# Reordering the prologue and one step of the per-chunk work in a two-part graph network kernel

## The chip, the cores and the metric

The kernel runs on one core of a Trainium2 chip. The metric is the device time of one execution in microseconds. The engines are named as in the profile: PE (TensorE; PEld is its weight load), DVE (VectorE), ACT (ScalarE), POOL (GpSimd) and SP (SyncE, which here only issues transfers). Each engine runs its own instructions in the order in which they are written; between engines there are only semaphore waits.

## What is computed

For each of 64 graphs of 128 nodes with 128 features (all float32), two blocks follow each other:

```
x1  = layernorm(x + L0(x, adj))          # L0: graph convolutions on nodes 0..24 only
out = layernorm(x1 + L1(x1, adj) * mask)

L0: w = softmax(fusion_w)
    for 5 groups g of nodes: A = adj_g + I, deg = rowsum(A), Ahat = deg^-1/2 A deg^-1/2
        h     = relu(Ahat (x_g W1[g]) + b1[g])
        out_g = relu(Ahat (h   W2[g]) + b2[g]);   fused[nodes of g] += w[g] * out_g
L1: A = (adj != 0); h = x1
    for 5 layers l: h = GRU( A^T (h weight[l]), h )      # gates r, z, n; w_ih, w_hh shared
```

## The kernel before

**Tiling.** The 64 graphs are cut into 4 chunks of 16, a chunk into 4 visits of 4 graphs (512 columns). L0 is done for a chunk at a time, L1 for a visit at a time. The main loop has 80 windows: 20 for each chunk (5 layers times 4 visits, the four visits in turn). `w.i` is the number of a window in its chunk (0 to 19). While the loop does L1 of one chunk, L0 of the next chunk is spread over its windows; class `Plan` says which step is done in which window. L0 of chunk 0 has no loop to hide in and stands in the prologue.

**A window.** PE multiplies the state of a visit by the hidden weights and the neighbours' sum by the fused weights `wf`, each as three products (high half by high half, low by high, high by low: L1063 to L1065), transposes the state that the window before the last has left (`turn`, L1050) and sums neighbours for a window to come (`aggregate`, L1057). ACT does the sigmoids and tanh and the high halves, POOL `dg` (L433), DVE `cg` (L889, L892), the new state `hT` (L830, L832) and the low halves (L818, L824). `turn` waits for the state of the window before the last, which DVE writes behind its L889 and L892 of the window before.

**L0 of a chunk, step by step.** DVE adds the adjacency rows up (`degrees`), POOL takes the power -1/2 (`power`), DVE scales (`scaled`), DVE (chunk 0) or POOL (`spread`) lays the block-diagonal matrices `bda` and `bdb` out. PE transposes them (`adjacency`), multiplies by x (`neighbours`), by W1 (`hidden_a`, `hidden_b`), by W2 (`second_a`, `second_b1`, `second_b2`) and by the adjacency again (`output_a`, `output_b`), ACT and DVE taking each result out of PSUM. `gather` adds the groups' parts into `fused` in 8 tensor_tensor instructions, each waiting for the one before it (DVE in the prologue, L746; POOL in the loop, L382). `back` transposes `fused` to rows (PE, L1026), `add` adds them to x (DVE, L756), and layer norm 1 follows: statistics on DVE (`norm1`, L763, L767), deviation on POOL (`deviation1`, L395 to L400), and the scaling on ACT, in the prologue for visit 0 half on DVE (`half_norm1`, L781) and for visits 2 and 3 on POOL. `ones` (POOL, L368) turns 4 graphs' adjacency in place into 0/1, from the 1 MB of `an` that SP loads for each chunk; the same loads bring `xn`.

**The prologue's weights.** `w_ih`, `w_hh` and `weight` are loaded, transposed on PE and copied by ACT (`wit`, `wh`, `wlt`). PE then multiplies `wlt[l]` by `wit` to give the fused weights of layer l (`fused_weights`, L936) in PSUM bank `WF_BANKS[l]`; ACT copies their high half (`high_weights`, L474), DVE subtracts for the low half (`low_weights`, L773). The loop uses banks P0 and P1 at once, P4 to P7 for states and sums. The softmax of `fusion_w` needs an exponential on ACT, whose activation tables hold either the exponential or the sigmoid; a tiny sigmoid (L560) loads the second set ahead of the loop.

**Orders by hand.** Every engine's prologue is a written-out list of these steps. SP issues the rows of `adj` and `x` for chunk 0, W1, W2, then chunk 0's `xn` and `an`, then the rows of `adj` for chunk 1. ACT issues its share of rows and then `w_ih`, `w_hh`, `weight`, the biases, the mask and `fusion_w`.

Of the kernel before, what the change touches and what calls it, by code (L numbers as in the profile page):

```python
# [7 lines left out]
NG = len(GROUPS)  # L8
# [70 lines left out]
class Plan:  # L79

    ADJ, Y, HA, HB, SA, SB, OA, OB, GATHER, BACK, REST = 2, 3, 4, 5, 6, 7, 8, 9, 10, 11, (12, 13)
    DEGREES, SCALED, SPREAD = 10, 12, 13
# [3 lines left out]
    STATS2 = {4: 0, 6: 1, 8: 2, 9: 3}  # L86
# [33 lines left out]
def build(nc, x, adj, nodemask, W1, b1, W2, b2, fusion_w, weight, w_ih, w_hh, b_ih, b_hh, out):  # L120
# [3 lines left out]
    with ctx:  # L124
# [75 lines left out]
        WF_BANKS = (1, 5, 6, 7, 0)  # L200
# [8 lines left out]
        def b1c(g, c):  # L209
# [4 lines left out]
        w_in, wl_in, w1_in, w2_in, xt_in, xt_pool_in, xa_in = map(sem, (  # L214
            "w_in", "wl_in", "w1_in", "w2_in", "xt_in", "xt_pool_in", "xa_in"))
# [62 lines left out]
        def _(sp):  # L278
# [4 lines left out]
            sp.dma_start(w1[:], W1.rearrange("g d h -> d g h")).then_inc(w1_in, 16)  # L283
# [39 lines left out]
        def _(pool):  # L323
# [103 lines left out]

# [20 lines left out]
        def _(act):  # L448
# [110 lines left out]
            high_weights(1)  # L559
            nc.scalar.activation(fmx[:], fmx[:], ACT.Sigmoid)  # L560
# [3 lines left out]
            for l in range(2, LAYERS):  # L564
                high_weights(l)
# [75 lines left out]
        def _(dve):  # L641
# [142 lines left out]
            degrees(0)  # L784
            dve.wait_ge(prep_hi, 1)
            TT(wh[:, 1, :], P[1][:, 0:GATES], wh[:, 0, :], ALU.subtract).then_inc(prep_lo, 1)
            scaled(0)
            adjacency(0)
            dve.wait_ge(w_in, 16 * 6)
            nc.vector.tensor_reduce(fmx[:], fw[:], AX.X, ALU.max, negate=True).then_inc(fw_ok, 1)  # L790
            neighbours(0)
            dve.wait_ge(exp_ok, 1)
            link(nc.vector.reciprocal(fsum[:], fsum[:]))
# [4 lines left out]
            hidden_b0(0)  # L798
            low_weights(0)
            second_b1(0)  # L800
            second_b2(0)
            low_weights(1)
            degrees(1)
            gather(0)
# [384 lines left out]
```

## Time and profile before

| | |
|---|---|
| median of 3 runs | 569.48 us (569.06 to 569.87) |
| the profiled execution | 569.57 us |
| its span in the profile | 567.3 us |
| busy: PE, DVE, ACT, POOL | 516.9, 443.0, 370.7, 257.7 us |
| mean granted TensorE clock | 0.97 of 2.4 GHz |
| loop: first product of window 0 | 52.01 us |

The span is divided into what each engine was busy with; an engine that is idle while another one sets the pace costs nothing. A row of a timeline gives start and duration in us, and in brackets the idle time of the engine before it and what ended it. The chain that ended last is followed back from the last instruction, so its rows in order of time tell what set the pace.

### The profile page before, as it was taken

Reading aid. Unit: us, or ns where it says so; the run is one execution under the profiler, and the core shown is the slowest. Engines: PE = TensorE matmul, PEld = TensorE weight load, DVE = VectorE, ACT = ScalarE, POOL = GpSimd, SP = SyncE. Lnnn points to the kernel's source line nnn. Section 1 sums busy time; section 2 is a strip of 40 time slices with the busy share of each in tenths; the row PEclk is TensorE's granted clock in tenths of the full one; section 3 lists DMA queues with packets and bytes.
Section 4 is the critical chain, followed back from the end, with each engine's and each line's share of the span. In section 5 each row is a group of like instructions: output and inputs, shape, how many; then the busy total and the mean of one; then the engine's idle time right before and its main releaser. Section 6 shows DMA issues by size and latency. Waiting matters only on the chain.

```text
span 567.3 us, 8362 instructions
## 1 busy us (share of the span) xinstructions
PE 516.9 (91%) x2907; PEld 434.7 (77%) x2907; DVE 443.0 (78%) x970; ACT 370.7 (65%) x682; POOL 257.7 (45%) x303
## 2 busy tenths in 40 slices
PE   1945999999999999998999999998999999999981
PEld 1734889887788788886788788887888888888860
DVE  3474667679998876888998877786998898887785
ACT  1433765675786765676787666676887767788644
POOL 5356523554554224666463323665254234442325
PEclk9985999999999999999999999998999999999995
DMA  4948610000000000000100000000000000000002
GB/s 106 233 134 198 155 27 8 1 1 0 1 1 1 1 25 7 20 1 20 39 1 1 0 1 2 20 0 20 18 20 2 1 1 1 19 20 27 12 0 74
DMA packets 35712, 17.27 MB, mean 30 GB/s; under 512 B 4429, under 2 KB 35648, under 8 KB 35672
## 3 DMA queue, kind: packets, MB, share of 16 engines
q1 hardware_dynamic: 33225, 15.78, 10.7%
q10 hardware_dynamic: 2063, 0.80, 0.6%
q8 instruction: 23, 0.38, 0.3%
q0 software_dynamic: 384, 0.17, 0.2%
q14 instruction: 17, 0.14, 0.1%
HBM read 12.54 MB, written 4.19 MB: 30 GB/s over the span
## 4 chain that ended last, share of the span: by engine, by line
PE 79%; DVE 8%; POOL 5%; ACT 3%; issue 2%; ACTq 1%; DMA 1%; POOLq 0%; DVEq 0%
PE p L1063 17%; PE p L1065 17%; PE p L1064 17%; PE p L1057 11%; PE p L1050 7%; PE p L981 3%; PE p L955 1%; POOL fused L382 1%; POOL an L368 1%; DVE cg L889 1%; PE p L974 1%; DVE cg L892 1%; DVE hT L832 1%; DMA zg<-in_L_gnn_weight_dram 1%; DVE dg L830 1%
## 5 line engine op out<-in xcount | busy, mean ns | idle before, releaser
L433 POOL TENSOR_TENSOR dg<-hT,ng 128x512 f32<-128x512 f32 x80 | 126.0, 1575 | 266.8 <-ACT ng L625 266.8
L1063 PE MATMUL p<-hhi,wh 128*128 128x512 f32 x240 | 102.3, 426 | 0.0
L889 DVE SCALAR_TENSOR_TENSOR cg<-p,biasc,rg 128x512 f32<-128x512 f32 x80 | 59.6, 745 | 54.5 <-ACT rg L612 54.1
L1063 PE MATMUL p<-ghi,wf 128*128 128x512 f32 x240 | 102.0, 425 | 0.0
L1064 PE MATMUL p<-hlo,wh 128*128 128x512 f32 x240 | 95.2, 397 | 0.0
L1065 PE MATMUL p<-hhi,wh 128*128 128x512 f32 x240 | 95.1, 396 | 0.0
L1065 PE MATMUL p<-ghi,wf 128*128 128x512 f32 x240 | 95.0, 396 | 0.0
L1064 PE MATMUL p<-glo,wf 128*128 128x512 f32 x240 | 95.0, 396 | 0.0
L612 ACT ACTIVATE rg<-p,gb 128x512 f32<-128x512 f32 x80 | 55.4, 693 | 33.5 <-PE p L1065 27.7
L818 DVE TENSOR_TENSOR hlo<-hT,hhi 128x512 fp32r<-128x512 f32 x76 | 72.4, 953 | 3.5 <-ACT hhi L636 0.6
L625 ACT ACTIVATE ng<-cg,biasc 128x512 f32<-128x512 f32 x80 | 57.9, 723 | 23.8 <-DVE cg L892 23.6
L1057 PEld LDWEIGHTS p<-an,nat 128*128 128x128 f32 x512 | 67.0, 191 | 5.8
L623 ACT ACTIVATE zg<-p,gb 128x512 f32<-128x512 f32 x80 | 55.0, 687 | 24.8 <-PE p L1065 24.6
L1057 PE MATMUL p<-an,nat 128*128 128x128 f32 x512 | 67.4, 274 | 0.0
L892 DVE TENSOR_TENSOR cg<-cg,p 128x512 f32<-128x512 f32 x80 | 55.0, 688 | 8.3
L824 DVE TENSOR_TENSOR glo<-p,ghi 128x512 fp32r<-128x512 f32 x80 | 55.3, 691 | 5.8 <-ACT ghi L581 5.8
L832 DVE TENSOR_TENSOR hT<-ng,dg 128x512 f32<-128x512 f32 x80 | 55.5, 694 | 2.8
L610 ACT COPY nat<-p 128x512 f32<-128x512 f32 x64 | 37.9, 592 | 28.8 <-PE p L1050 27.6
L1050 PE MATMUL p<-ident,hT 128*128 128x128 f32 x320 | 50.1, 280 | 6.9 <-DVE hT L832 6.9
L830 DVE TENSOR_TENSOR dg<-zg,dg 128x512 f32<-128x512 f32 x80 | 55.0, 688 | 0.0
L1065 PEld LDWEIGHTS p<-hhi,wh 128*128 128x128 f32 x240 | 45.3, 189 | 11.1
L1065 PEld LDWEIGHTS p<-ghi,wf 128*128 128x128 f32 x240 | 45.3, 189 | 11.0
(128 smaller groups left out, 832.8 us busy)
## 6 DMA issues: line engine op xcount, KB each, us to landing
xn<-in_x_dram SPq DMA_DIRECT2D x8, 512.0 KB, 5.2
an<-in_adj_dram SPq DMA_DIRECT2D x8, 512.0 KB, 7.1
out_dram<-xn SPq DMA_DIRECT2D x16, 256.0 KB, 2.3
w<-in_L_gnn_W_dram SPq DMA_DIRECT2D x2, 640.0 KB, 5.4
xt<-in_x_dram SPq DMA_DIRECT2D x16, 50.0 KB
zg<-in_L_gnn_weight_dram ACTq DMA_DIRECT2D x1, 320.0 KB, 5.6
xt<-in_x_dram SPq DMA_DIRECT2D x8, 36.0 KB
xt<-in_x_dram SPq DMA_DIRECT2D x12, 24.0 KB
```

What stands on the lines that cost most here:

```text
L433: nc.gpsimd.tensor_tensor(dg[:, w.k % 2, :], hT[:, w.slot, :], ng[:, w.k % 2, :], ALU.subtract).then_inc(d_ok, 1)
L625: nc.scalar.activation(ng[:, p, :], cg[:, p, :], ACT.Tanh, bias=bin_).then_inc(n_ok, 1)
L818: TT(hlo[:, m % SLOTS, :], hT[:, m % SLOTS, :] if source is None else source[:], hhi[:, m % SLOTS, :], ALU.subtract).then_inc(lo_ok, 1)
L830: TT(dg[:, p, :], zg[:, p, :], dg[:, p, :], ALU.mult).then_inc(e_ok, 1)
L832: TT(hT[:, s, :], ng[:, p, :], dg[:, p, :], ALU.add).then_inc(h_ok, 1)
L889: STT(cg[:, p, :], PH[:], bhn, rg[:, p, :], ALU.add, ALU.mult).then_inc(t1_ok, 1)
L892: TT(cg[:, p, :], cg[:, p, :], PI[:], ALU.add).then_inc(c_ok, 1)
L1050: last = TR(bank[:, q * 128:(q + 1) * 128], src(q), ident[:])
L1057: last = MM(bank[:, q * N:(q + 1) * N], src(q), an[:, b + q, :], start=True, stop=True)
L1063: MM(bank[:], w[:, 0, cols], xhi, start=start, stop=False)
L1064: MM(bank[:], w[:, 0, cols], xlo, start=False, stop=False)
L1065: return MM(bank[:], w[:, 1, cols], xhi, start=False, stop=stop)
```

## The change

`Plan`: `back` moves from window 11 to 12, the rest of `add` from 12 and 13 to 13 and 14, `degrees` (and `power`) from 10 to 11, `scaled` from 12 to 13, `spread` from 13 to 14, and one statistics step of layer norm 2 from window 9 to 10.

Prologue, by engine:
- SP no longer issues W1; ACT issues it behind `weight`. POOL issues the mask. ACT issues `fusion_w` first. The waits are split: PE's first transposes wait for `w_ih` and `w_hh` alone.
- ACT does the exponential and the tiny sigmoid first, then the copies; `high_weights(0)` goes behind `second_a(0)`, `high_weights(1)` to (4) behind `output_b(0)`; `maskc` is copied behind `second_a(0)`.
- DVE takes the low half of `wh` behind `adjacency(0)`; the `low_weights` go between and behind the steps of `add` and `norm1`, one behind `lo_state(0)`; `scaled(1)` goes behind `norm1(3)`.
- POOL does `ones(0)` and `ones(1)` ahead of `power(1)`, `ones(2)` and `ones(3)` behind it, `spread(1)` last.
- PE transposes `wl` and the biases' rows behind `adjacency(0)`; `fused_weights(0)` goes behind `second_b2(0)`, (1) and (2) behind `output_b(0)`, (3) and (4) behind `back(0)`.

```diff
-    ADJ, Y, HA, HB, SA, SB, OA, OB, GATHER, BACK, REST = 2, 3, 4, 5, 6, 7, 8, 9, 10, 11, (12, 13)
-    DEGREES, SCALED, SPREAD = 10, 12, 13
+    ADJ, Y, HA, HB, SA, SB, OA, OB, GATHER, BACK, REST = 2, 3, 4, 5, 6, 7, 8, 9, 10, 12, (13, 14)
+    DEGREES, SCALED, SPREAD = 11, 13, 14
...
-    STATS2 = {4: 0, 6: 1, 8: 2, 9: 3}
+    STATS2 = {4: 0, 6: 1, 8: 2, 10: 3}
...
-        WF_BANKS = (1, 5, 6, 7, 0)
+        WF_BANKS = (1, 0, 5, 4, 7)
...
@@ sync
-            sp.dma_start(w1[:], W1.rearrange("g d h -> d g h")).then_inc(w1_in, 16)
...
@@ gpsimd
             power(0)
             spread(0)
+            pool.dma_start(maskr[:], nodemask).then_inc(mask_in, 16)
             pool.wait_ge(ac_zero, 2)
             load_adj_rows(pool, 1, TA, ac_pool_in[1])
+            ones(0)
+            ones(1)
             power(1)
-            spread(1)
-            for visit in range(SLOTS):
-                ones(visit)
+            ones(2)
+            ones(3)
             deviation1(0)
             deviation1(1)
             for visit in (2, 3):
                 deviation1(visit)
                 norm1(visit)
+            spread(1)
...
@@ scalar, loads
+            act.dma_start(fw[:], fusion_w.partition_broadcast(128)).then_inc(fw_in, 16)
+            act.dma_start(wir, ...).then_inc(gates_in, 16)
+            act.dma_start(whr, ...).then_inc(gates_in, 16)
             act.dma_start(wl, weight.rearrange("l c e -> c l e")).then_inc(wl_in, 16)
+            act.dma_start(w1[:], W1.rearrange("g d h -> d g h")).then_inc(w1_in, 16)
...
@@ scalar, steps (new order)
+            act.wait_ge(fw_ok, 1); exp; sigmoid
+            copy wit; copy wh high (prep_hi)
+            adjacency(0)
+            copy wlt (wlt_ok); copy biasc (prep_a)
+            neighbours(0); hidden_a(0); hidden_b1(0); second_a(0)
+            copy maskc; high_weights(0)
+            output_a(0); output_b(0)
+            high_weights(1..4)
...
@@ vector (new order)
+            degrees(0)
+            dve.wait_ge(fw_in, 16); reduce max of fw (fw_ok)
+            scaled(0)
+            adjacency(0)
+            dve.wait_ge(prep_hi, 1); wh low (prep_lo)
+            dve.wait_ge(exp_ok, 1); reciprocal; fw scaled
+            neighbours(0); gb; fb2 (b_ok)
+            hidden_b0(0); second_b1(0); second_b2(0)
+            degrees(1)
+            gather(0)
+            low_weights(0)
+            add(0, True); norm1(0)
+            low_weights(1)
+            add(0, False); half_norm1(0, HALVES[1])
+            low_weights(2)
+            norm1(1)
+            low_weights(4)
+            lo_state(0, PL)
+            low_weights(3)
+            lo_neighbours(0, PG)
+            norm1(2); norm1(3)
+            scaled(1)
+            lo_state(1, PM)
...
@@ tensor (new order)
+            pe.wait_ge(gates_in, 32); transposes of wir, whr
+            adjacency(0)
+            transposes of wl (wait wl_in); transpose of rows (wait w_in, wlt_ok)
+            neighbours(0); hidden_a(0); hidden_b(0); second_a(0)
+            transpose of maskr
+            second_b1(0); second_b2(0)
+            fused_weights(0)
+            output_a(0); output_b(0)
+            fused_weights(1); fused_weights(2)
+            back(0)
+            fused_weights(3); fused_weights(4)
```

The lists of ACT, DVE and PE above stand for the moved lines; the helpers that they call are unchanged. The waits of `prep_lo` on PE follow the new order of the low halves.

## Rows read from the trace of the kernel before

**Rows 1.** Busy time of each engine in the profile's page, with shares and instructions.

```profile
PE 516.9 (91%) x2907; PEld 434.7 (77%) x2907; DVE 443.0 (78%) x970; ACT 370.7 (65%) x682; POOL 257.7 (45%) x303
```

**Rows 2.** Timeline of PE: start, us, instruction; in brackets idle before, releaser.

```profile
13.54 1.06 PE L925 MATMUL p<-ident,zg 128*128 128x128 f32 x4
...
49.22 1.09 PE L1050 MATMUL p<-ident,xn 128*128 128x128 f32 x4 [12.61 <-ACT xn L532]
...
260.26 0.66 PE L1026 MATMUL p<-ident,fused 128*128 128x128 f32 x4 [2.25 <-POOL fused L382]
...
389.35 1.06 PE L1026 MATMUL p<-ident,fused 128*128 128x128 f32 x4 [2.08 <-POOL fused L382]
```

**Rows 3.** The chain that ended last, in order of time: start, us, what.

```profile
15.25 1.48 DVE bda L696 x4
...
18.42 1.33 PE p L936 x2
...
38.77 7.59 POOL an L368 x4
...
48.24 0.89 ACT xn L532 x2
...
52.01 0.59 PE p L1063
```

**Rows 4.** Timeline of DVE in the prologue.

```profile
14.29 0.56 DVE L786 TENSOR_TENSOR wh<-p,wh 128x384 fp32r<-128x384 f32 x1 [4.80 <-ACT wh L465]
...
31.08 0.38 DVE L672 TENSOR_TENSOR am<-ac,member 128x225 f32<-128x225 f32 x1
...
33.37 2.47 DVE L746 TENSOR_TENSOR fused<-fused,part 128x72 f32<-128x72 f32 x8 [0.56 <-ACT part L522]
...
36.73 1.21 DVE L756 TENSOR_TENSOR xn<-xn,p 25x128 f32<-25x128 f32 x4
...
39.29 2.29 DVE L756 TENSOR_TENSOR xn<-xn,p 25x384 f32<-25x384 f32 x4
```

**Rows 5.** Stretches of whole windows: busy (x count) by engine, clock, DMA share, GB/s.

```profile
121.96:168.78 46.82, 46.40 (x248) 36.95 (x246) 44.28 (x97) 32.44 (x57) 26.40 (x35) 1.00 0.00 1
249.93:298.00 48.07, 45.81 (x248) 37.05 (x246) 43.97 (x97) 36.71 (x69) 28.52 (x40) 1.00 0.06 18
379.16:428.10 48.94, 46.86 (x247) 38.80 (x246) 42.03 (x89) 36.56 (x69) 23.89 (x33) 0.97 0.06 17
501.83:540.54 38.71, 38.71 (x213) 32.65 (x212) 30.37 (x43) 29.87 (x52) 11.13 (x7) 1.00 0.07 21
151.83:168.78 16.95, 16.95 (x94) 13.64 (x92) 15.90 (x43) 13.54 (x27) 10.42 (x17) 1.00 0.00 1
...
384.91:394.79 9.88, 7.80 (x37) 6.43 (x36) 5.57 (x12) 5.05 (x10) 4.81 (x9) 0.83 0.10 28
```

**Rows 6.** Timelines of POOL and of SP's queue in the prologue.

```profile
9.49 1.83 POOL L338 TENSOR_TENSOR dinv<-deg,minus_half 128x9 f32<-128x9 f32 x1 [2.00 <-DVE deg L681]
...
19.97 7.14 SPq L246 DMA_DIRECT2D ac<-in_adj_dram  x8
```

**Rows 7.** Timeline of ACT in the prologue.

```profile
14.63 0.59 ACT L467 COPY cg<-p 128x512 f32<-128x512 f32 x1 [0.37 <-PE p L925]
...
30.59 1.28 ACT L560 ACT_TABLE_LOAD   x1
```

**Rows 8.** Short stretches ahead of and in window 0, with columns as in rows 5.

```profile
26.00:27.00 1.00, 1.00 (x12) 1.00 (x11) 0.12 (x1) 0.60 (x3) 0.00 (x0) 1.00 0.13 13
...
52.01:54.95 2.94, 2.94 (x8) 2.28 (x8) 2.25 (x12) 2.61 (x6) 0.23 (x2) 0.50 0.91 208
54.95:60.11 5.16, 5.16 (x37) 4.59 (x35) 2.87 (x9) 3.55 (x6) 4.65 (x11) 1.00 0.08 9
```

**Rows 9.** Timelines of POOL and DVE in window 1 of chunk 2.

```profile
193.84 1.63 POOL L433 TENSOR_TENSOR dg<-hT,ng 128x512 f32<-128x512 f32 x1 [3.72 <-ACT ng L625]
...
194.25 1.77 DVE L818 TENSOR_TENSOR hlo<-hT,hhi 128x512 fp32r<-128x512 f32 x1
```

More of the change, by code:

```diff
@@ L563, in _ @@
             output_b(0)
-            for l in range(2, LAYERS):
+            for l in range(1, LAYERS):
                 high_weights(l)
@@ L782, in half_norm1 @@
                 last.then_inc(ln1_dve, 1)
[L784 to L793, printed above, removed]
-            link(TS(fw[:], fw[:], fsum[:], None, ALU.mult))
-            dve.wait_ge(prep_a, 1)
-            TT(gb[:], biasc[:, BI:BI + 2], biasc[:, BI + 3:BI + 5], ALU.add)
-            TT(fb2[:], biasc[:, NG * HC:BI], fw[:], ALU.mult).then_inc(b_ok, 1)
[L798 to L804, printed above, removed]
-            scaled(1)
-            low_weights(2)
-            add(0, True)
-            norm1(0)
-            add(0, False)
-            half_norm1(0, HALVES[1])
-            norm1(1)
-            low_weights(3)
-            low_weights(4)
             def lo_state(m, source=None):
@@ L852, in norm2 @@
                 last.then_inc(ln2_st, 1)
+            degrees(0)
+            dve.wait_ge(fw_in, 16)
+            nc.vector.tensor_reduce(fmx[:], fw[:], AX.X, ALU.max, negate=True).then_inc(fw_ok, 1)
+            scaled(0)
+            adjacency(0)
+            dve.wait_ge(prep_hi, 1)
+            TT(wh[:, 1, :], P[1][:, 0:GATES], wh[:, 0, :], ALU.subtract).then_inc(prep_lo, 1)
+            dve.wait_ge(exp_ok, 1)
+            link(nc.vector.reciprocal(fsum[:], fsum[:]))
+            link(TS(fw[:], fw[:], fsum[:], None, ALU.mult))
+            neighbours(0)
+            dve.wait_ge(prep_a, 1)
+            TT(gb[:], biasc[:, BI:BI + 2], biasc[:, BI + 3:BI + 5], ALU.add)
+            TT(fb2[:], biasc[:, NG * HC:BI], fw[:], ALU.mult).then_inc(b_ok, 1)
+            hidden_b0(0)
+            second_b1(0)
+            second_b2(0)
+            degrees(1)
+            gather(0)
+            low_weights(0)
+            add(0, True)
+            norm1(0)
+            low_weights(1)
+            add(0, False)
+            half_norm1(0, HALVES[1])
+            low_weights(2)
+            norm1(1)
+            low_weights(4)
             lo_state(0, PL)
+            low_weights(3)
             lo_neighbours(0, PG)
@@ L1029, in _ @@
             adjacency(0)
-            pe.wait_ge(prep_lo, 1)
-            fused_weights(0)
+            pe.wait_ge(wl_in, 16)
+            for l in range(4):
+                last = TR(P[2][:, l * 128:(l + 1) * 128], wl[:, l, :], ident[:])
+            last.then_inc(prep_t, 1)
+            TR(P[3][:, 0:128], wl[:, 4, :], ident[:]).then_inc(prep_t, 1)
+            nr = NG * HC + NG + 6
+            pe.wait_ge(w_in, 16 * 4)
+            pe.wait_ge(wlt_ok, 1)
+            TR(P[3][:, 128:128 + nr], rows[:], ident[0:nr, 0:nr]).then_inc(prep_t, 1)
             neighbours(0)
@@ L1125, in _ @@
                 if k == 0:
+                    pe.wait_ge(prep_lo, 5)
                     enter(1, PM)
```

61 lines of the change are left out of this document (27 added, 34 removed).

## The prediction

> **What bounds the kernel now.** I read the page's busy shares first: PE is busy 516.9 of 567.3 us [rows 1], so a gain must come from stretches in which PE stands idle. I then listed PE's idle stretches by their releaser [rows 2]. Before the loop PE first idles about 12 us, then works until 36.6 us, and then idles 12.61 us until ACT has normalised the first visit. In the loop it waits 2.25 and 2.08 us at `back` (L1026) for the additions of `gather` on POOL; at the first chunk's `back` it does not wait. Third, the chain of waits in order of time [rows 3]: it goes through DVE's `bda`, the product of layer 0's weights on PE, and from 38.77 on through four `ones` on POOL (7.59 us) and the deviation behind them, until ACT starts on `xn` at 48.24. So before the loop POOL's order sets the end. Fourth, DVE's own order [rows 4] shows what comes into play once POOL is out of the way. Last, windows 10 to 17 of each chunk in the loop [rows 5], since the change moves steps among them.
>
> **The changed prologue.** All times are new positions on the old clock.
>
> DVE now waits 4.80 us for ACT's `wh`, only to subtract it, ahead of `scaled(0)` [rows 4]. POOL's `power(0)` ends at 9.49 + 1.83 = 11.3 [rows 6]. With the subtraction moved behind, `scaled(0)` runs from 11.4 to 13.35: 1.95 us, as from 14.8 (behind `wh`) to 16.73 [rows 3, 4]. PE's `adjacency(0)` takes 1.7 us (16.73 to 18.42 [rows 3]), so to 15.0. What is new between it and `neighbours(0)`: the transposes of `wl`, 1.06 and about 0.3 us [rows 2], ACT's copies of them (0.59 us and a shorter one, about 0.8 with waits [rows 7]) and the transpose of the rows: 2.2 us, to 17.2. It was 18.42 + 1.33 = 19.75 [rows 3], so 2.5 us are gained. Against that, `fused_weights(0)` (0.7) now stands ahead of `output_a`, in the place that `fused_weights(1)` had: nothing. ACT's table load of 1.28 us, at 30.59 right before `output_a` [rows 7], moves into the time before 13 us, where ACT waits anyway. The first addition of `gather(0)` can then start at 33.37 - 2.5 - 1.28 = 29.6 instead of 33.37 [rows 4]; `output_b` on PE, 2.5 us earlier, and ACT's first `part` behind it make it 30.0, and I keep 0.8 for a slow start of PE: 30.0 to 30.8.
>
> The order before `gather(0)` on DVE is still `degrees(1)`. Its rows of `adj` are issued by SP from 19.97 to 27.11 [rows 6]; W1's 640 KB leave SP for ACT's queue, which puts SP 0.5 to 2 us ahead, so they land at 26.5 to 28.1. DVE is free at 27.7 to 28.5. So `degrees(1)` is ready at about 28.1 and needs 1.75 us (31.08 to 33.37 less the 0.56 idle [rows 4]).
>
> POOL: chunk 0's loads end at about 26.4 (DMA share 0.13 in the slice from 26 [rows 8]). W1 out of their way takes up to 2 us off; I take 25.0. `ones(0)`, `ones(1)` at 7.59/4 = 1.9 each end at 28.8, `power(1)` (1.83 like `power(0)` [rows 6]) waits for `degrees(1)`, and `ones(2)`, `ones(3)` come after. Without contention they end at 35.5, before DVE has the statistics, so POOL is off the chain.
>
> **The cost the trace hardly shows.** `degrees(1)` and `gather(0)` are tensor_tensor with both inputs in SBUF, and they now run beside `ones`, where before POOL was idle or in a `pow` of 9 columns. The nearest row: a DVE tensor_tensor with two SBUF inputs that starts 0.41 us into a POOL tensor_tensor takes 1.77 us and ends 0.55 us after it [rows 9]: it is held until POOL's instruction is over. For `ones`, with one input, no row shows a DVE instruction of this kind starting inside. Lower bound: no hold, `gather` runs 30.8 to 33.2. Upper bound: each is held for all that is left of a `ones`. I take the hold, since the row is of the same engines and the same direction. Then `degrees(1)` runs 28.9 to 30.65 and `power(1)` 30.6 to 32.4; five or six of the eight additions are done by then, one is held by `ones(2)` to 34.4, and since each addition waits for the one before it, POOL takes `ones(3)` next, to 36.5. The last two end at 36.8, not 33.2: 3.6 us given back. Bounds for this end: 35.4 (loads at 24.2) and 38.0 (loads at 26.4).
>
> The Trainium skill ("SBUF — State Buffer", section "Who interferes with whom") says that DVE and GpSimd share a port pair as an exclusive lock, that a DVE instruction with two SBUF inputs contends with any GpSimd instruction that reads SBUF, and that whoever starts first blocks the other for the whole instruction. By that rule `ones` belongs with the held case; the trace agrees for tensor_tensor with its 1.77 us, and shows nothing for `ones`.
>
> Behind the additions: from their end 0.9 us to `add` (33.37 + 2.47 = 35.84 to 36.73), which covers `back` and `low_weights(0)`; then to the end of `add(0, False)` 39.29 + 2.29 - 36.73 = 4.85, and 0.5 for `low_weights(1)`, which now stands between [rows 4]. So DVE comes to its half of `norm1(0)` at 36.8 + 6.25 = 43.05, where it started at 48.24. POOL's deviation (46.4 to 48.24, 1.8 us) starts after the statistics at 40.3 and ends at 42.1: hidden. Now DVE is the last, not POOL. From there DVE's work to `lo_state(0)` is the same amount (one half norm, `norm1(1)`, two `low_weights`), so the first product of window 0 comes 3.8 us later as now (48.24 to 52.01 [rows 3]), at 46.9 instead of 52.01: **-5.1 us**. `low_weights(3)` (0.5) fits DVE's wait for `ghi`. `scaled(1)` and `spread(1)` (2.4 on POOL, ahead of window 0's `dg`) end ahead of `adjacency(1)` in window 2; `dg` is late by some 0.5 us for DVE, which has waits of over 1 us there: **+0.2**, at most 1.
>
> PE restarts at 1.2 GHz as now: the granted clock is 0.50 until 54.95, 5.7 us after the restart [rows 2, 8], and PE's idle time ahead of it remains some 5 us. A rise earlier or later by some us costs half of that: +-1.5 for the range.
>
> **The loop.** A window in which nothing is late takes 38.71/7 = 5.53 us. Windows 10 to 17 would take 8 x 5.53 + 0.5 for `back` = 44.7; they took 46.82, 48.07 and 48.94 [rows 5]. DVE's own work in a window is 4.5 us: in windows 15 to 17, 16.95/3 = 5.65 with the 1.2 of a norm1 (add's start to 39.29 less its 1.21 is 1.35 with gaps) [rows 4, 5]. Where a window's DVE work passes about 5.6, PE ends up waiting for hT at the turning of the next one. So I added up each window's DVE work and let PE wait for what it is late. `back` a window later removes both waits for POOL, 2.25 and 2.08, and the half clock behind the second (window 11 took 9.88 us at 0.83 [rows 5]; 5.53 + 0.5 + 2.08 = 8.1 at full clock): 6.0 us. But the same DVE work is now pushed into fewer windows: window 10 has only a norm2 or nothing, and window 14 has half of the rest of `add` (1.15) and a norm1 (1.2), 6.85 us in all, for which PE waits 1.3. `spread` in window 14 behind POOL's deviation (2.8 us) also makes `dg` and the next deviation 0.7 late, through ACT's norm1 and zg 0.4 for PE, and about 0.3 by holding DVE. Window by window: chunk 1: 5.75, 5.53, 6.03, 5.71, 6.15, 6.86, 5.68, 6.06 = 47.8 (+1.0); chunk 2: 5.75, 5.67, 6.17, 5.74, 6.15, 6.86, 5.68, 6.06 = 48.1 (0); chunk 3, without `degrees` and `scaled`: 5.75, 5.67, 6.03, 5.53, 5.53, 6.47, 5.68, 5.68 = 46.3 (-2.6). With 0.3 twice for `spread`: **-1.0 us**; bounds -6.0 (nothing given back) and +1.5. The other moves (a norm2 from window 9 to 10) lie in waits of over 1 us.
>
> **Sum.** -5.1 + 0.2 - 1.0 = -5.9. The profiled execution took 569.57 (span 567.3, 2.3 around it), the median is 569.48: **563.6 us**.
>
> **Rivals.**
> - *No hold by `ones`.* Additions end at 33.2, half norm at 39.45, window 0 at 43.3: -8.7 + 0.2 - 1.0, 560.0 us. For it: `pow` beside the additions did not hold them. Against it: rows 9. Chance 0.17.
> - *The waits at `back` vanish and nothing is given back*: 569.5 - 5.1 + 0.2 - 6.0 = 558.6 with the hold. Against it: 5.65 in windows 15 to 17 shows DVE at its limit. Chance 0.08.
> - *DVE is held at every turn*, loads as late as now, and chunk 1's windows slow down as bounded: additions end at 38.0, -3.9 + 1 + 1.5: 568.1. Chance 0.05 (with a part beyond the bound of 0.2%).
> - *The slower side: the clock.* If after the restart PE stays at 1.2 GHz for more windows, each costs up to its 5.53 us once more, since PE is busy throughout it: about 5. From 1.2 such windows on the gain of 5.9 is gone; two give 573.6. Against it: the same instructions raised it after 5.7 us. Chance 0.04.
> - The forecast, 0.66; within it earlier or later loads and clock.
>
> **Range and chances.** 558.5 to 567.0 takes in the first two rivals and leaves out about 1 in 10. The forecast's own range is 561.5 to 566. A difference of 0.2% (1.1 us) is about what a measurement of this kernel tells from none. Faster 0.93, within 0.03, slower 0.04.
>
> **What would show it.** Right: `bda` ends near 13.4; `neighbours(0)` starts on PE near 17.2; one or two of DVE's additions in the prologue take 1 to 2 us, ending with a `ones`; DVE, not POOL, ends the wait before `norm1(0)`; window 0's first product near 47; no PE idle ahead of `back` in the loop; window 15 near 6.9. Wrong: additions all below 0.4 us (first rival); window 15 at 5.6 (second); a granted clock of 0.50 past 53 us (fourth); or `neighbours(0)` waiting for `xt`, which W1 on ACT's queue could make late: it is due at 17.2.

## The result, and the profile after

The changed kernel takes 564.61 us (median of 4 runs, 564.47 to 564.89), the kernel before, run beside it, 569.53 us: a ratio of 0.9901 (95% interval 0.9877 to 0.9926; it isn't the quotient of the two medians, which is 0.9914). The forecast was 563.6. The profiled execution of the changed kernel took 564.52 us, its span is 562.6.

The busy line of its page answers to [rows 1]:

```profile
PE 519.8 (92%) x2907; PEld 434.3 (77%) x2907; DVE 447.4 (80%) x970; ACT 371.0 (66%) x682; POOL 259.5 (46%) x304
```

PE's timeline after the change, with the columns of [rows 2]:

```profile
17.59 0.29 PE L1027 MATMUL p<-ident,rows 21*128 21x21 f32 x1 [1.34 <-DMA rows<-in_L_gnn_b_hh_dram]
17.81 2.03 PE L944 MATMUL p<-na,xt 100*128 100x100 f32 x8
...
21.76 2.65 PE L953 MATMUL p<-ya,w 128*128 128x400 f32 x4
...
36.69 0.63 PE L1015 MATMUL p<-ident,fused 128*128 128x128 f32 x4 [2.24 <-DVE fused L747]
...
43.41 1.09 PE L1052 MATMUL p<-ident,xn 128*128 128x128 f32 x4 [3.98 <-DVE xn L782]
...
46.23 0.77 PE L1065 MATMUL p<-hhi,wh 128*128 128x512 f32 x1
...
63.35 0.52 PE L933 MATMUL p<-ident,bda 100*100 100x100 f32 x4 [1.64 <-DVE hlo L788]
```

The 12.61 us that PE waited for ACT [rows 2] have become 3.98 us for DVE. Window 0's first product starts at 46.23; in this view it started at 51.84 before (the chain of [rows 3] puts it at 52.01). The waits of 2.25 and 2.08 us at `back` are gone: the loop has no idle time of PE there any more. What came in instead is the last row: 1.64 us in window 2.

DVE's timeline (`add` is L757, `gather` L747, `half_norm1` L782, the state hT L802):

```profile
31.08 0.38 DVE L673 TENSOR_TENSOR am<-ac,member 128x225 f32<-128x225 f32 x1
...
33.74 2.80 DVE L747 TENSOR_TENSOR fused<-fused,part 128x72 f32<-128x72 f32 x8 [0.94 <-ACT part L515]
...
37.43 1.22 DVE L757 TENSOR_TENSOR xn<-xn,p 25x128 f32<-25x128 f32 x4 [0.42 <-PE p L1015]
...
42.68 0.58 DVE L782 TENSOR_SCALAR xn<-xn,rs,nm 128x128 f32<-128x128 f32 x2
...
60.37 1.67 DVE L802 TENSOR_TENSOR hT<-ng,dg 128x512 f32<-128x512 f32 x1
```

POOL's timeline (`ones` is L367, `power` L337, the end of `spread` L358, `dg` L435):

```profile
27.03 3.85 POOL L367 TENSOR_SCALAR an<-an 128x512 f32<-128x512 f32 x2 [10.49 <-DMA an<-in_adj_dram]
32.81 1.83 POOL L337 TENSOR_TENSOR dinv<-deg,minus_half 128x9 f32<-128x9 f32 x1 [1.92 <-DVE deg L682]
34.63 3.81 POOL L367 TENSOR_SCALAR an<-an 128x512 f32<-128x512 f32 x2
...
56.83 1.55 POOL L358 TENSOR_TENSOR bdb<-am,ksel 72x144 f32<-72x144 f32 x5
58.32 1.28 POOL L435 TENSOR_TENSOR dg<-hT,ng 128x512 f32<-128x512 f32 x1
60.03 1.45 POOL L435 TENSOR_TENSOR dg<-hT,ng 128x512 f32<-128x512 f32 x1 [0.42 <-ACT ng L626]
```

`gather` lies wholly beside `power` and `ones`, as foreseen, and yet its eight additions take 2.80 us instead of 2.47: they are not held for a whole `ones`.

Stretches of whole windows, with the columns of [rows 5]: windows 0 and 2, then windows 10 to 17 ahead of chunk 1, 15 to 17 of these, and 10 to 17 ahead of chunks 2 and 3:

```profile
46.23:53.85 7.62, 7.62 (x43) 6.61 (x43) 5.89 (x23) 6.15 (x12) 5.12 (x13) 0.89 0.82 216
...
59.38:67.45 8.07, 6.43 (x43) 5.33 (x41) 6.53 (x12) 5.46 (x12) 1.68 (x2) 1.00 0.71 186
117.18:165.93 48.75, 46.95 (x248) 36.91 (x246) 45.87 (x97) 32.51 (x57) 26.91 (x35) 1.00 0.00 1
146.76:165.93 19.17, 17.77 (x94) 13.49 (x92) 18.22 (x48) 13.62 (x27) 13.07 (x21) 1.00 0.00 1
247.09:295.97 48.88, 47.09 (x247) 36.86 (x246) 46.46 (x105) 36.79 (x69) 29.34 (x40) 1.00 0.06 17
377.13:423.46 46.33, 45.76 (x247) 37.25 (x246) 43.50 (x97) 36.70 (x69) 24.03 (x33) 1.00 0.06 18
```

Against the 46.82, 48.07 and 48.94 of [rows 5] that is +1.93, +0.81 and -2.61: the loop as a whole comes out even. The difference of the two spans splits as follows: prologue 51.84 to 46.23, -5.61; window 0 from 8.27 to 7.61, -0.66; window 2 from 6.59 to 8.07, +1.48; windows 10 to 17, +0.13. Together -4.66, of the 4.7 between 567.3 and 562.6. So between these two executions all of the gain is the prologue's, and the plan brings nothing. Experiment 2 adds a reservation to the second half, and experiments 1 and 5 show that the prologue's share is understated here.

### The profile page after: what moved, and what is told of

It reads as the page before. It is cut to its first block, busy times and chain, and to the rows that moved or that the text cites. A ratio compares the mean times of both kernels' runs of the same rounds, so it can differ in the third digit from the quotient of the medians.

```text
span 562.6 us, 8366 instructions
## 1 busy us (share of the span) xinstructions
PE 519.8 (92%) x2907; PEld 434.3 (77%) x2907; DVE 447.4 (80%) x970; ACT 371.0 (66%) x682; POOL 259.5 (46%) x304
## 4 chain that ended last, share of the span: by engine, by line
PE 68%; DVE 16%; POOL 6%; ACT 4%; issue 3%; ACTq 2%; DMA 1%; DVEq 0%; POOLq 0%
PE p L1065 14%; PE p L1067 14%; PE p L1066 14%; PE p L1059 9%; PE p L1052 6%; PE p L970 3%; DVE hT L802 2%; DVE cg L889 2%; DVE cg L892 2%; DVE xn L757 2%; DVE dg L800 2%; PE p L944 2%; PE p L963 1%; DMA rows<-in_L_gnn_b_hh_dram 1%; POOL dg L435 1%
## 5 line engine op out<-in xcount | busy, mean ns | idle before, releaser
L435 POOL TENSOR_TENSOR dg<-hT,ng 128x512 f32<-128x512 f32 x80 | 125.3, 1566 | 264.5 <-ACT ng L626 264.5
L788 DVE TENSOR_TENSOR hlo<-hT,hhi 128x512 fp32r<-128x512 f32 x76 | 75.8, 998 | 3.8 <-ACT hhi L637 0.6
L802 DVE TENSOR_TENSOR hT<-ng,dg 128x512 f32<-128x512 f32 x80 | 56.5, 706 | 2.8
L1052 PEld LDWEIGHTS p<-ident,hT 128*128 128x128 f32 x320 | 37.4, 143 | 23.8 <-DVE hT L802 18.8
L1065 PEld LDWEIGHTS p<-hhi,wh 128*128 128x128 f32 x240 | 45.6, 190 | 13.0 <-DVE cg L889 3.6
L1067 PEld LDWEIGHTS p<-hhi,wh 128*128 128x128 f32 x240 | 45.3, 189 | 11.0
```

The source lines that it names most:

```text
L435: nc.gpsimd.tensor_tensor(dg[:, w.k % 2, :], hT[:, w.slot, :], ng[:, w.k % 2, :], ALU.subtract).then_inc(d_ok, 1)
L788: TT(hlo[:, m % SLOTS, :], hT[:, m % SLOTS, :] if source is None else source[:], hhi[:, m % SLOTS, :], ALU.subtract).then_inc(lo_ok, 1)
L802: TT(hT[:, s, :], ng[:, p, :], dg[:, p, :], ALU.add).then_inc(h_ok, 1)
L1052: last = TR(bank[:, q * 128:(q + 1) * 128], src(q), ident[:])
L1065: MM(bank[:], w[:, 0, cols], xhi, start=start, stop=False)
L1067: return MM(bank[:], w[:, 1, cols], xhi, start=False, stop=stop)
```

## The experiments

The kernel before took 569.8 us beside experiments 1 to 4 (its executions range from 569.22 to 574.15), 570.17 beside 5 to 8 and 569.75 beside 9 to 12. Ratios are to it.

**1 and 2. Each half alone.** The kernel before with the new `Plan`, and the changed kernel with the old one (`STATS2` goes with it).

```diff
-    GATHER, BACK, REST = ..., 10, 11, (12, 13)      # experiment 1; experiment 2 is the other way round
-    DEGREES, SCALED, SPREAD = 10, 12, 13
+    GATHER, BACK, REST = ..., 10, 12, (13, 14)
+    DEGREES, SCALED, SPREAD = 11, 13, 14
```

> The kernel before with the new Plan alone; its prologue is untouched. If the loop's account of the trace after holds (windows 10 to 17 of the three chunks +1.9, +0.8 and -2.6 us), the change of the loop is worth nothing by itself: 569.6 us, within 0.5 of before. If instead the removed waits at back are a gain that something of the new prologue took away again, it takes 563.5 to 565.

> The changed kernel with the old Plan. If the parts add up, the prologue is the whole gain: 564.5 us, with the waits of 2.2 and 2.1 us ahead of back in the loop again and window 0's first product near 46.2. If the prologue needs the new Plan (a slower first chunk), 567 or more.

The plan alone: 572.09 us, 1.0023 (0.9996 to 1.0051), which is not told apart from no change, though the median is 2.3 us above the one expected at most 0.5 away. The prologue alone: 565.45 us, 0.9909 (0.9877 to 0.9942), where 564.5 was expected. With the plan alone windows 10 to 17 take 48.77, 48.88 and 46.33 us, as in the changed kernel: +0.15 in all, and the profiled execution is longer than the kernel before only by its prologue, whose instructions are the same. There window 0 starts at 53.82 instead of 51.84. PE's timeline of experiment 1 shows why:

```profile
19.46 1.87 PE L955 MATMUL p<-na,xt 100*128 100x100 f32 x8
21.12 2.33 PE L955 MATMUL p<-nb,xt 72*128 72x72 f32 x10
23.25 2.44 PE L964 MATMUL p<-ya,w 128*128 128x400 f32 x4
...
53.82 0.77 PE L1063 MATMUL p<-hhi,wh 128*128 128x512 f32 x1
```

In the kernel before the same three rows take 1.64, 1.28 and 1.54 us. By these durations PE came up to its full clock some 4 us later: in the kernel before at about 20.8, here at about 25.1. So an execution's prologue can be 2 us longer or shorter with no change to the code ahead of it, and that difference must not be read as an effect of the plan.

The same holds for the prologue's gain. The kernel before was profiled in an execution in which the clock rose at about 20.8, the changed kernel in one in which it rose at about 24.0, so the -5.61 compares an early rise with a late one. Of the profiled executions, experiment 1 (the old prologue, rise at about 25.1) is matched by experiment 5, whose edit acts only behind the start of window 0 and whose clock rose at about 25.0. PE's timeline of experiment 5:

```profile
21.71 2.93 PE L953 MATMUL p<-ya,w 128*128 128x400 f32 x4
24.43 2.22 PE L963 MATMUL p<-yb,w 128*128 128x144 f32 x16
...
46.67 0.76 PE L1065 MATMUL p<-hhi,wh 128*128 128x512 f32 x1
```

53.82 against 46.67: with the rise at the same time, the new prologue is worth 7.15 us. This is one execution of each; at which time the clock rose in the others isn't known.

In experiment 2 window 0 starts at 46.34. Its loop keeps both waits at `back`, and the clock was at half behind both of them, where in the kernel before it was so behind the second alone:

```profile
256.00:260.00 4.00, 4.00 (x15) 3.35 (x14) 1.88 (x5) 2.04 (x4) 2.57 (x2) 0.57 0.00 0
...
385.50:389.50 4.00, 3.71 (x14) 3.30 (x15) 1.13 (x4) 1.01 (x2) 1.46 (x2) 0.57 0.00 0
```

Windows 10 to 17 ahead of chunk 2 take 49.13 there instead of 48.07, and the three groups together 144.86, 0.90 more than in the changed kernel. The new plan takes the waits and the half clock behind them away: the changed kernel runs at 1.00 from 47.9 to 549.7 us. So the plan costs 0.13 us against an execution with one such stretch and saves 0.9 against one with two. The medians (565.45 and 564.61, intervals overlapping) don't decide what it is worth on average.

**3. `spread` a window earlier.**

```diff
-    DEGREES, SCALED, SPREAD = 11, 13, 14
+    DEGREES, SCALED, SPREAD = 11, 13, 13
```

> The changed kernel with spread back in window 13, all else as changed. Windows 15 to 17 take 19.2 us in chunk 1 and 19.2 in chunk 2, but 17.9 in chunk 3, which has no spread. Theory: spread behind POOL's deviation in window 14 costs that difference, so they fall to 17.9: 562.1 us. Rival: the difference is DVE's lateness from degrees and scaled in windows 11 and 13; then they stay at 19.2: 564.6 us.

563.15 us, 0.9866 (0.9827 to 0.9905). Stretches of windows 10 to 17 of chunk 1, 15 to 17 of it, and 10 to 17 of chunk 2:

```profile
117.15:165.00 47.85, 46.53 (x248) 36.98 (x246) 44.81 (x97) 32.44 (x57) 26.56 (x35) 1.00 0.00 1
146.74:165.00 18.26, 17.32 (x94) 13.56 (x92) 17.14 (x48) 13.53 (x27) 10.41 (x17) 1.00 0.00 1
246.16:294.13 47.97, 46.61 (x248) 36.90 (x246) 45.39 (x105) 36.72 (x69) 29.02 (x40) 1.00 0.06 18
```

0.90 us less ahead of chunk 1 and 0.91 ahead of chunk 2, nothing ahead of chunk 3, where there is no `spread`. So `spread` behind the deviation in window 14 costs 0.9 us a time. In the changed kernel its `bdb` takes 2.43 us there, an `hlo` of DVE 1.63 instead of about 1.0, and ACT's `norm1` waits 1.03 us for POOL. The expectation had the place right and the size too high (17.9 for windows 15 to 17, which take 18.26). The rest over 17.88 of chunk 3 stands in window 15, as its rival had it: 6.96 us against 6.59. The interval of the time overlaps that of the changed kernel; the gain is read from the windows.

**4 and 5. Window 2.** What comes ahead of `dg` on POOL at the start of the loop: `spread(1)` behind window 0's `dg` (4), or ahead of the deviations of visits 2 and 3 (5).

```diff
@@ gpsimd, experiment 4
                 norm1(visit)
-            spread(1)
 
             for w in ALL_WINDOWS:
                 ...
                 nc.gpsimd.tensor_tensor(dg[:, w.k % 2, :], ...).then_inc(d_ok, 1)
+                if w.k == 0:
+                    spread(1)
@@ gpsimd, experiment 5
+            spread(1)
             for visit in (2, 3):
                 deviation1(visit)
                 norm1(visit)
-            spread(1)
@@ vector, experiment 5
             lo_neighbours(0, PG)
+            scaled(1)
             norm1(2); norm1(3)
-            scaled(1)
```

> The changed kernel with the prologue's spread(1) moved behind window 0's dg on POOL. Theory: the 1.64 us that PE waits ahead of adjacency(1) in window 2 come from dg being late behind spread(1), and from the next dg then holding DVE's hT (1.67 us instead of 0.69). Then hT takes 0.69 again and window 2 falls from 8.07 to 6.6 us: 563.1 us. Rival: spread(1) only moves the holding, and DVE's two tensor_tensor of window 1 are held by it: window 2 stays near 8, 564.6 us.

> The changed kernel, with scaled(1) on DVE one place earlier (behind lo_neighbours(0)) and spread(1) on POOL ahead of the deviations and norm1 of visits 2 and 3. Window 2 takes 8.07 us in the changed kernel (6.59 before): POOL's dg of window 0 starts only when spread(1) is over, and then dg of window 1 holds DVE's hT. Theory: with spread(1) early, dg of window 0 starts about 0.7 us sooner, DVE's hT of window 1's state is under way before the next dg starts and takes 0.7 us instead of 1.67, and window 2 takes 6.6: 563.1 us, 1.5 less than the changed kernel's 564.6. Rival: spread(1) pushes norm1(2) and norm1(3) on POOL back by its 2.4 us, DVE's or PE's work on visits 2 and 3 is late instead, and windows 0 to 3 together take what they took: 564.6.

Experiment 4: 564.72 us, 0.9892 (0.9854 to 0.9929); window 2 takes 7.92. Window 0's `dg` did start 2 us earlier, but DVE's hT was held as before. DVE and POOL in window 2:

```profile
59.49 0.95 DVE L801 TENSOR_TENSOR dg<-zg,dg 128x512 f32<-128x512 f32 x1
60.47 1.78 DVE L803 TENSOR_TENSOR hT<-ng,dg 128x512 f32<-128x512 f32 x1
```

```profile
60.41 1.30 POOL L434 TENSOR_TENSOR dg<-hT,ng 128x512 f32<-128x512 f32 x1 [0.52 <-ACT ng L627]
```

POOL's `dg` of window 1 started 0.06 us ahead of hT, because `spread` had held the instruction before hT for 0.26. The theory fell: it is not how late window 0's `dg` is, but which of the two instructions starts first.

Experiment 5: 565.32 us, 0.9915 (0.9900 to 0.9930). DVE and PE:

```profile
61.99 0.69 DVE L802 TENSOR_TENSOR hT<-ng,dg 128x512 f32<-128x512 f32 x1
```

```profile
54.73 0.63 PE L1052 MATMUL p<-ident,xn 128*128 128x128 f32 x4 [1.30 <-POOL xn L389]
```

hT takes 0.69 us and window 2 6.59, as the theory said (hT starts first: POOL's `dg` of window 1 follows at 62.19); and window 0 takes 9.33 instead of 7.61, as the rival said, since `norm1(2)` is 2.2 us later and PE waits 1.30 us for it. The two cancel. POOL has no gap between 48.6 and 59.5 us, and `spread(1)` costs about 1.5 us in either place.

**6. W1 behind the small rows.**

```diff
@@ scalar, loads
-            act.dma_start(w1[:], W1.rearrange("g d h -> d g h")).then_inc(w1_in, 16)
             ... rows ...
+            act.dma_start(w1[:], W1.rearrange("g d h -> d g h")).then_inc(w1_in, 16)
```

> The changed kernel, with ACT issuing W1 behind the small rows (biases, fusion weights) instead of ahead of them. In the changed kernel PE waits 1.34 us ahead of neighbours(0) for these rows, whose transfer took 7.11 us from issue to landing. Theory: the rows land before PE wants them, neighbours(0) starts near 16.5 instead of 17.8, and the chain behind it (to gather at 33.74) is about 0.8 us earlier, less than 1.3 because PE is still at 1.2 GHz for a time: 563.8 us. Rival: what ends the wait at gather, the rise of the clock or the loads of an and xn behind it, does not move: 564.6.

564.02 us, 0.9892 (0.9875 to 0.9908), which no measurement here tells from the changed kernel's 564.61. PE's timeline:

```profile
16.89 0.27 PE L1027 MATMUL p<-ident,rows 21*128 21x21 f32 x1 [0.72 <-ACT cg L551]
17.09 2.03 PE L944 MATMUL p<-na,xt 100*128 100x100 f32 x8
```

The wait for the rows is gone, and `neighbours(0)` starts 0.72 us earlier. Window 0 starts at 45.80, 0.43 earlier: the clock rises when it rose in the changed kernel (at about 24), so the products behind `neighbours(0)` run at half clock for longer (those of L953 take 2.93 us instead of 2.65), and about half of the 0.72 is given back.

**7 and 8. What holds DVE in the prologue.** All four `ones` ahead of `power(1)` (7); three added POOL instructions with two inputs in SBUF beside `gather(0)` (8). Nothing is left out.

```diff
@@ gpsimd, experiment 8
             ones(2)
+            for i in range(3):
+                a4 = an[:, i * SB:(i + 1) * SB, :]
+                nc.gpsimd.tensor_tensor(dg0, a4, a4, ALU.mult)      # dg0: dg[:, 0] seen as 4 blocks
             ones(3)
             deviation1(0)
+            power(1)
```

The waits of the added instructions for `ones(2)` and for one another are left out of this cut; `power(1)` is gone from its old place behind `ones(1)`.

> The changed kernel, with all four ones of chunk 0 on POOL in one run ahead of power(1), so that degrees(1) and gather(0) on DVE lie wholly beside ones. It asks whether a ones (one input from SBUF, 1.9 us) holds a DVE tensor_tensor with two inputs in SBUF. Theory of the prediction (held until the ones is over): degrees(1) or one or two of the eight additions take 1 to 2 us each. Rival, what the changed kernel's trace suggests: none is held, all take 0.20 to 0.40 us. Time 564.6 in both, by the rival, and up to 1.5 more by the theory.

> The changed kernel, with three added POOL instructions of 128x512, tensor_tensor with both inputs in SBUF, behind ones(2), where DVE does gather(0); ones(3) and power(1) go behind them. Nothing is left out; the added results are used by nobody. Theory: two inputs on each side are what makes an instruction wait, so additions of gather(0) that start inside such a POOL instruction take up to 1.6 us, the additions end 2 to 4 us later than the changed kernel's 36.5, and the time is 566 to 568 us. Rival: in the prologue nothing is held, whatever POOL does, the additions take 0.2 to 0.4 us, and only POOL's own delay of 1 to 2 us is seen, if anything: 564.6 to 565.5.

Experiment 7: 564.86 us, 0.9911 (0.9897 to 0.9926). Its `ones` run from 26.91 to 34.53 without a gap; DVE's `degrees(1)` lies inside, from 31.51, and takes what it takes elsewhere, but for one instruction of 0.48 us. The additions, by the view of the tile `fused`:

```profile
L745 DVE TENSOR_TENSOR fused<-fused,part x8: 185/216/321, 34.2 to 36.4; 128x48 f32<-128x48 f32 x4, 128x72 f32<-128x72 f32 x2, 128x16 f32<-128x16 f32 x1, 128x96 f32<-128x96 f32 x1
```

The longest addition takes 0.32 us. But only the first, at 34.18, lies beside a `ones`: the others stand beside `power(1)`, which ran from 34.51 to 36.34. So for `ones` it is `degrees(1)` that counts here: two tensor_tensor of 225 columns with both inputs in SBUF took 0.38 and 0.40 us inside. In the changed kernel the last four additions, from 35.51 on, lie beside `ones(2)` and take 0.21 and 0.22 us, as they did in the kernel before with POOL idle. Experiment 8: 566.42 us, 0.9935 (0.9920 to 0.9949). Its POOL instructions and DVE's timeline beside them:

```profile
32.59 3.28 POOL L427 TENSOR_TENSOR dg<-an 128x512 f32<-128x512 f32 x3
```

```profile
32.72 0.94 DVE L690 TENSOR_TENSOR deg<-deg,zero 128x9 f32<-128x9 f32 x1
...
33.91 4.11 DVE L755 TENSOR_TENSOR fused<-fused,part 128x72 f32<-128x72 f32 x8 [0.17 <-ACT part L523]
```

An addition of 9 columns took 0.94 us instead of 0.17: it started 0.13 us into a POOL instruction of 1.04 us and ended with it. Two of the additions of `gather` took 0.99 and 1.01 us. The additions end at 38.0 instead of 36.5 (2 to 4 us later was expected), window 0 starts at 48.16, 1.93 later, and the time is 1.8 us longer, within what the theory gave. So a POOL tensor_tensor of 512 columns holds DVE and a `ones` of 512 columns does not. That the number of inputs makes the difference fits, but isn't shown: the two differ in the kind of instruction too, and `power(1)`, a tensor_tensor of 9 columns with two SBUF inputs that takes 1.83 us, did not hold the additions of 0.29 us beside it, before, after or in experiment 7.

**9 to 12. Toward a better version.** SPREAD 13 and W1 behind the rows together (9). W1 behind the rows with another plan (10). Experiment 9 with 9 added products on PE that nobody reads (11), and experiment 10 with them (12).

```diff
@@ Plan, experiments 10 and 12
-    GATHER, BACK, REST = ..., 10, 12, (13, 14)
-    DEGREES, SCALED, SPREAD = 11, 13, 14
-    STATS2 = {4: 0, 6: 1, 8: 2, 10: 3}
+    GATHER, BACK, REST = ..., 10, 12, (12, 13)
+    DEGREES, SCALED, SPREAD = 10, 11, 12
+    STATS2 = {4: 0, 6: 1, 8: 2, 9: 3}
@@ tensor, experiments 11 and 12
+            pe.wait_ge(oa_ok, 1)
+            for _ in range(3):
+                MM(P[2][:, 0:COLS_A], w1[:, 0, 0:128], ya[:], start=True, stop=True)
             back(0)
             fused_weights(3); fused_weights(4)
+            for _ in range(6):
+                MM(P[2][:, 0:COLS_A], w1[:, 0, 0:128], ya[:], start=True, stop=True)
```

> The changed kernel with the two edits that helped alone: SPREAD in window 13, and W1 issued behind the small rows. The first took 1.7 us off the span, the second 0.3 off the span and 0.4 off the start of window 0. They touch different stretches. Theory: they add, 562.6 us. Rival: spread in window 13 or the clock's rise takes the small gain back, 563.2.

> W1 behind the rows, and another plan: BACK 12, REST (12, 13), DEGREES 10, SCALED 11, SPREAD 12, STATS2 with window 9 for visit 3. So only back moves from the kernel before, and what DVE has to do for it is spread again. Theory: windows 10 to 17 are set by DVE's work of each window and what it is late for the next; adding that up window by window gives 47.4 for chunk 1 where the same sum gives 47.4 for the changed plan, 47.2 instead of 47.8 for chunk 2 and 45.9 instead of 46.3 for chunk 3, and spread away from window 14 gives 0.9 in each of two chunks: 1.0 us less than the kernel with SPREAD 13, 561.6. Rival: window 12, which now carries add, half of its rest and back, becomes the long one, since POOL's spread stands there too and holds DVE: no gain over SPREAD 13 alone, 562.6 or above.

> The kernel with SPREAD 13 and W1 behind the rows, with 9 added products of 400 columns on PE in the prologue, whose result nobody reads: 3 ahead of back(0), 6 behind fused_weights(4), where PE stood idle for 2.2 and 4.0 us. In all runs the granted clock fell to 0.50 in these waits and rose only 1.7 us or more into window 0. Theory: PE has no long idle time, so the clock stays at 1.00; enter(0) and aggregate take 1.6 instead of 3.0 us, but DVE's lo_state(0) then sets the start of window 0, which comes at most 0.3 earlier, and window 0 takes 1 us less: 0.8 to 1.2 us less than without, 561.6. Rival: the clock falls all the same, or the added products delay back or enter, and the time is as without or 0.5 above, 562.6 to 563.1.

> The other plan, W1 behind the rows and the 9 added products together. If each does what its theory says: 560.6 us. If neither does: 562.6. The plan acts in windows 9 to 19, the products before window 1, so what each brings alone should add.

Experiment 9: 562.55 us, 0.9868 (0.9847 to 0.9889), as its theory said. Its profiled execution got there by another way in part: the clock rose late, window 0 started at 46.75 and took 8.20 us, and POOL's `dg` of window 1 started at 61.14, behind hT at 60.94, so that hT was not held and window 2 took 6.59.

Experiment 10: 564.48 us, 0.9899 (0.9879 to 0.9920). Windows 10 to 17 take 48.64, 49.72 and 45.93 us: only the 45.93 ahead of chunk 3 is as added up. DVE's timeline and the stretch of chunk 2:

```profile
259.86 0.17 DVE L689 TENSOR_TENSOR dinv<-dinv,zero 128x9 f32<-128x9 f32 x1 [3.22 <-POOL dinv L337]
...
264.85 2.37 DVE L757 TENSOR_TENSOR xn<-xn,p 25x128 f32<-25x128 f32 x6
```

```profile
246.57:296.29 49.72, 46.68 (x248) 36.92 (x246) 43.97 (x97) 36.71 (x69) 28.48 (x40) 1.00 0.06 17
```

`scaled` in window 11 waits 3.22 us for the power that POOL takes behind its other work of window 10, and DVE's queue stands behind it; in window 12 DVE then has six additions of `add` in a row. Adding up DVE's work had left out that a step can wait. The rival named window 12; the wait in window 11 was in neither.

Experiment 11: 561.36 us, 0.9849 (0.9825 to 0.9873), span 558.6. PE's timeline, and window 0:

```profile
18.94 1.54 PE L953 MATMUL p<-ya,w 128*128 128x400 f32 x4
...
36.65 4.19 PE L1053 MATMUL p<-ya,w 128*128 128x400 f32 x12
41.61 0.63 PE L1057 MATMUL p<-ident,xn 128*128 128x128 f32 x4 [0.77 <-DVE xn L782]
...
44.42 0.48 PE L1070 MATMUL p<-hhi,wh 128*128 128x512 f32 x1 [1.10 <-DVE hlo L788]
```

```profile
44.42:51.61 7.19, 7.07 (x42) 5.95 (x43) 5.77 (x23) 5.71 (x11) 5.10 (x13) 1.00 0.81 212
```

The rows that DVE's `degrees(1)` needs land later than PE's work, by DVE's timeline:

```profile
30.06 0.50 DVE L673 TENSOR_TENSOR am<-ac,member 128x225 f32<-128x225 f32 x1 [2.84 <-DMA ac<-in_adj_dram]
```

With PE busy through its waits the granted clock stays at 1.00 from before 18.94 to 544.95 us. As expected, DVE's `lo_state(0)` then sets the start of window 0 (the 1.10 us), and window 0 is 0.4 to 1.0 shorter. But of the 2.33 us by which window 0 starts earlier than in experiment 9, nearly all was there before the first added product: L953 takes 1.54 us here and 2.93 in experiment 9, at half clock. The runs of experiment 11 range from 560.49 to 562.94, and its interval overlaps that of experiment 9, so the gain of 1.2 us in the medians isn't established. The profiled execution is the fastest of its five. Experiment 12: 564.14 us, 0.9896 (0.9873 to 0.9920), 0.3 below experiment 10 where 1.0 was expected. In its profiled execution, the fastest of six, the clock rose early too. The expectation's "in all runs" (a rise 1.7 us or more into window 0) has an exception: in experiment 8 it came 0.2 us into it.

The best version is the changed kernel with SPREAD 13 and W1 behind the rows: 562.55 us, or 561.36 with the added products; the intervals of experiments 3, 9 and 11 overlap.

## Why the prediction was right, step by step

The sum was -5.1 + 0.2 - 1.0 = -5.9; the spans show -5.61 + 0.82 + 0.13 = -4.66. The direction, the prologue as the source and the end of it were right. Inside, errors cancelled, so that the total is right in part by luck: a late start of `gather` against a hold that didn't come, and a better prologue (7.15 with the clock's rise alike, experiments 1 and 5) against a later rise and a plan that brought nothing.

- *DVE's early steps.* `bda` ends at 12.99 (forecast 13.4), as foreseen.
- *The start of `neighbours(0)`*, 17.2 forecast, is 17.81. PE waited 1.34 us for the last of the small rows, 7.11 us under way. I had seen that W1 on ACT's queue could make a load late, but named the wrong one. Experiment 6 shows it.
- *The first addition of `gather(0)`*, forecast for 30.0 to 30.8, starts at 33.74, later than the 33.37 of before. This is the step that failed. From the two timelines: `neighbours(0)` 1.74 earlier; its products and those of L953 2.47 slower; 0.35 for what now stands between them and `output_a`, the mask's transpose among it; and 0.71 saved between `output_a` and `gather`, where I had counted the table load's whole 1.28 though part of it lay beside PE's product. -1.74 + 2.47 + 0.35 - 0.71 = +0.37. The 2.47 has two parts, by an estimate from the timelines. PE was at half clock up to about 20.8 before and up to about 24.0 after. What it is ahead in that stretch is worth half once the clock is up: 0.87 of the 1.74 is lost. And the 3.2 us by which the rise came later cost half of that, 1.6. The first part belongs to the change: experiment 1 and experiment 5 rise at the same time, `neighbours(0)` starts 1.70 earlier (17.76 for 19.46), L970 only 0.83 earlier than its counterpart (26.49 for 27.32), and `gather` 1.2 earlier (34.19 for 35.37). The second part is a difference of executions that no run ties to the change. I had allowed 0.8 for a slow start of PE.
- *The rows of `adj` for `degrees(1)`*, forecast to land at 26.5 to 28.1, would have stopped it too. SP issued them until 28.8 instead of 27.1. In experiment 11, where PE was at full clock from the start of `neighbours(0)` on, DVE waited 2.84 us for them, to 30.06, and `gather` started at 31.85. So 30.0 to 30.8 was out of reach even at full clock.
- *Chunk 0's loads*, forecast to end at 25.0, let POOL start on `ones` at 27.03. Taking W1 off SP didn't put SP ahead: its issues of `xn` and `an` took 9.73 us instead of 7.30, while W1 was under way on ACT's queue and POOL's loads stood 3.1 us earlier than before (which of the two did it is open), and the rows of `adj` behind them were issued from 21.91 instead of 19.97.
- *The hold by `ones`* (3.6 us given back) did not happen. One addition took 0.66 us, the others 0.2 to 0.3. The row it was taken from [rows 9] has two inputs and 512 columns on either side; with POOL's instruction of that form the additions were held, with a `ones` they were not (experiments 7 and 8). The Trainium skill ("SBUF — State Buffer", section "Who interferes with whom") says that a DVE instruction with two SBUF inputs contends with a GpSimd instruction that reads SBUF. For tensor_tensor against POOL's tensor_tensor of 512 columns the runs agree (0.94 us for 0.17); for `ones`, which reads SBUF too (0.22 us beside it, 0.22 without), and for the `power` of 9 columns (0.29 us beside it), they do not.
- *The end of the additions*, forecast 36.8, is 36.5: 3 us of late start in place of 3.6 us of hold. A right number by two wrong terms: luck. From there on the sum held: half norm at 42.68 (43.05), DVE last and not POOL, the deviation hidden, window 0's first product at 46.23 (46.9).
- *Rival one*, no hold and 560.0 us, had its mechanism right and its time wrong, since it kept the early start of `gather`. Its condition, all additions below 0.4 us, was met but for the one of 0.66.
- *Windows 0 to 2*: +0.2 and at most 1 was forecast for `spread(1)` and `dg`. The clock gave 0.66 back (it rose 4.5 us after PE's restart, 5.7 before), and window 2 cost 1.48. I had priced the delay of `dg`, not that it would start just ahead of hT and hold it: 1.67 us instead of 0.69. The row for it was there [rows 9]. Experiments 4 and 5.
- *The loop*: chunk 3 is -2.61 where -2.6 was forecast. Window 15 takes 6.95 and 6.97 us, forecast 6.9: DVE's late work in window 14 costs what was said. Chunks 1 and 2 are 48.75 and 48.88 where 47.8 and 48.1, with 0.3 for `spread` in each, stood. `spread` costs 0.9 and not 0.7 in all (experiment 3), window 12, with the first `add`, takes 6.45 and 6.43 us and not 6.03 and 6.17, and window 15 gives the last 0.1. So the term had its mechanism right and its size wrong: +0.13 and not -1.0.

## What to carry to other kernels

A step that is moved earlier brings only what the next limit lets through: list for each stage of a prologue the latest of its inputs, transfers included, and treat the time at which PE's clock rises as a quantity of its own that does not come with the work: here 1.7 us of lead gained ahead of the rise were worth 0.8 behind it. Before two profiled executions are subtracted, look whether the clock rose at the same place in both. Where two engines can hold one another, ask not how late an instruction becomes but which of the two then starts first. When a plan spreads steps over windows, add up the engine's work and the waits of each step for the step before it on the other engine; here a wait of 3.22 us undid a plan whose sums were right.

## What the runs showed of the hardware that was not expected

- POOL's tensor_scalar on one SBUF input (128x512, 1.9 us) does not hold DVE's tensor_tensor on two: four additions beside it take 0.21 and 0.22 us in the changed kernel, two instructions of 225 columns 0.38 and 0.40 in experiment 7. POOL's tensor_tensor of 128x512 on two inputs holds it to its end: 0.94 instead of 0.17 us (experiment 8), 1.78 instead of 0.69 (experiment 4). POOL's tensor_tensor of 128x9 (`power`, 1.83 us) does not: 0.29 us beside it. What tells the forms apart was not tested further.
- Close behind the start of a `ones` single DVE instructions took 0.3 to 0.45 us more: 0.66 at 34.76 in the changed kernel, with a `ones` from 34.63; 0.66 instead of 0.22 at 33.84 in experiment 11, with one from 33.83; 0.48 instead of 0.17 in experiment 7, a tensor_scalar with one input. Why is open.
- The same early instructions of PE ran at half clock or at full in different executions: the four products of 400 columns took 1.54 us (before, experiments 11 and 12), 2.44 (experiment 1), 2.65 (after) and 2.93 (experiments 6 and 9). It is worth 2 us of the kernel's time. In these first 24 us the granted clock in the view of stretches reads 1.00 whatever the durations say. What decides the time of the rise was not settled: ahead of it the instructions of experiments 9 and 11 are the same. The only two profiled executions of the new prologue with an early rise are those of the two kernels with added products, which stand some 13 us behind the rise; one execution each doesn't show whether that is chance.
- SP's issue of the two 512 KB transfers of `xn` took 5.32 us with W1 on ACT's queue and POOL's loads early, and 3.78 us with W1 ahead of them on SP's own queue. The next such pair, at 38.12, took 1.05.
